# Two GpSimd instructions at other places, and the last returned rows taken in halves

## The reference

```
x = x + 0.5 * L0_ffn(layernorm(x))        # 8 experts, dense
x = x + L0_attn(layernorm(x))             # landmark attention
x = x + 0.5 * L0_ffn(layernorm(x))
x = x + 0.5 * L1_ffn(layernorm(x))        # 32 experts, top 4, plus a shared expert
x = x + L1_attn(layernorm(x), ...)        # windows of 128, half overlapping
x = x + 0.5 * L1_ffn(layernorm(x))
```

```
scores = softmax(flat @ router_w.T + router_bias)
topk_scores, topk_idx = top_k(scores, 4)                 # normalised over the 4
expert_out = (silu(gate_e x) * (up_e x)) @ down_e.T      # only the chosen 4 count
out = sum over the 4 of topk_score * expert_out
out = out + (silu(x @ sgate.T) * (x @ sup.T)) @ sdown.T  # the shared expert
```

## Time and profile before

| | us |
|---|---|
| median of 3 runs | 802.93 |
| lowest, highest | 802.22, 803.98 |
| the profiled execution | 803.43 |
| its span | 801.9 |

### The profile page before, as it was taken

How to read it: one execution, slowest core, us unless ns; L and a number is a source line. 1 busy time by engine, 2 the same in 40 slices (tenths; PEclk the granted TensorE clock), 3 DMA queues, 4 the chain that set the end, 5 groups by cost and what they waited for, 6 DMA issues and landing times.

```text
span 801.9 us, 19539 instructions
## 1 busy us (share of the span) xinstructions
PE 709.4 (88%) x6738; PEld 545.6 (68%) x6738; DVE 549.9 (69%) x1651; ACT 398.9 (50%) x967; POOL 442.8 (55%) x484
## 2 busy tenths in 40 slices
PE   7979998888999998898988889889968987988986
PEld 6868865556997756787777555557756775555655
DVE  6887477766886637987788745557588778555464
ACT  3656755565642553665652355562535423565531
POOL 4754560035650002655567677777237777777772
PEclk9998999999999999999999799999989898999999
DMA  8999999939003907300112454444301123444473
GB/s 226 206 204 202 203 200 207 214 84 205 6 4 67 165 2 268 126 1 33 40 46 66 117 130 113 113 119 145 119 12 48 45 67 99 108 112 112 110 230 112
DMA packets 121024, 93.99 MB, mean 117 GB/s; under 512 B 14176, under 2 KB 111840, under 8 KB 120544
## 3 DMA queue, kind: packets, MB, share of 16 engines
q1 hardware_dynamic: 104256, 70.00, 40.7%
q0 software_dynamic: 9216, 19.68, 7.1%
q10 hardware_dynamic: 7456, 3.07, 1.9%
HBM read 31.76 MB, written 57.41 MB: 111 GB/s over the span
## 4 chain that ended last, share of the span: by engine, by line
PE 37%; DVE 26%; issue 11%; POOL 11%; ACT 8%; ACTq 3%; DMA 3%; DVEq 0%; POOLq 0%; SPq 0%
PE banks L2046 6%; POOL sorted_rows L467 5%; POOL expert_rows L836 4%; PE banks L1424 3%; ACT routed_scratch L857 3%; DVE hT L1333 2%; PE banks L1027 2%; DVE rows_x L218 2%; DMA tile<-sorted_rows 2%; PE banks L414 2%; PE banks L416 2%; PE banks L415 2%; ACTq L894 2%; PE banks L1042 2%; POOL rstd L211 1%
## 5 line engine op out<-in xcount | busy, mean ns | idle before, releaser
L836 POOL DMA_INDIRECT expert_rows<-y,goal x160 | 154.5, 966 | 48.8 <-issue 46.2
L467 POOL DMA_INDIRECT sorted_rows<-rows_x,row_of x128 | 127.3, 995 | 66.1 <-issue 36.3
L1292 ACT ACTIVATE ys<-banks,wtab 128x128 f32<-128x128 f32 x256 | 73.3, 370 | 66.0 <-PE banks L1424 54.8
L1027 PE MATMUL banks<-routed_w,t 128*64 x320 | 82.2, 402 | 2.7 <-DVE t L921 1.8
L414 PE MATMUL banks<-x_high,w_high 128*128 128x512 f32 x192 | 83.9, 437 | 0.2 <-POOL w_low L1171 0.2
L1218 POOL TENSOR_TENSOR x<-ys,x 128x512 f32<-128x512 f32 x43 | 55.0, 1278 | 50.7 <-ACT ys L1292 50.4
L938 DVE TENSOR_TENSOR h<-sg,banks 128x512 f32<-128x512 f32 x40 | 27.5, 687 | 80.5 <-ACT sg L866 62.6
L1027 PE MATMUL banks<-routed_scratch,t 128*64 128x256 f32 x320 | 82.4, 403 | 0.0
L1424 PE MATMUL banks<-w,hT 128*128 128x128 f32 x512 | 71.7, 284 | 10.9 <-DVE hT L1333 10.7
L1424 PEld LDWEIGHTS banks<-w,hT 128*128 128x128 f32 x512 | 65.8, 195 | 19.8 <-issue 11.5
L211 POOL TENSOR_TENSOR rstd<-rstd,mhalf 128x4 f32<-128x4 f32 x24 | 26.7, 1114 | 91.9 <-DVE rstd L205 91.7
(11 more groups left out here) (361 smaller groups left out, 1717.2 us busy)
## 6 DMA issues: line engine op xcount, KB each, us to landing
sorted_rows<-zeros SPq DMA_DIRECT2D x32, 1120.0 KB, 17.9
tile<-sorted_rows SPq DMA_DIRECT2D x252, 35.0 KB
routed_w<-in_ffn_w SPq DMA_DIRECT2D x8, 768.0 KB, 11.9
w<-in_ffn_w SPq DMA_DIRECT2D x20, 192.0 KB, 5.2
routed_scratch<-expert_rows SPq DMA_DIRECT2D x3, 1024.0 KB, 5.7
expert_rows<-y,goal POOLq DMA_INDIRECT x160
tile<-sorted_rows ACTq DMA_DIRECT2D x68, 35.0 KB
qS<-x_high SPq DMA_DIRECT2D x8, 256.0 KB, 5.7
```

What stands on the lines that cost most here:

```text
L467: POOL.indirect_dma_start(sorted_rows, bass.IndirectOffsetOnAxis(self.row_of[:, g, i:i + 1], 0), rows_x[:, 4 * g + i // TOPK, :], None).th ...
L836: POOL.indirect_dma_start(expert_rows, bass.IndirectOffsetOnAxis(goal[:, 4 * q + i:4 * q + i + 1], 0), y[q % 6][:, i * P:(i + 1) * P], Non ...
L1027: last = PE.matmul(pairs(q)[ROWS * h:ROWS * h + ROWS, i, :], t[q % 2][:, rows], weights(q, i, h, slice(0, 2 * P)), start=True, stop=True)
L1292: last = SCL.mul(ys[s % 2][:, j * P:(j + 1) * P], bank[4 + s % 2][:, j * P:(j + 1) * P], wtab[:, t, e:e + 1])
```

## The change

Three things are changed, all of them in the stages after 567 us.

1. In `attn1`, POOL's `pool_pair(3)` stands ahead of `srt.norm.power(0)` and no longer behind it.
2. `pool_dispatch(1, 1)` becomes `pool_dispatch(1, 3)`: the power of group 2 stands behind three of group 1's indirect DMAs, not behind one.
3. In the second `Sorted`, the last group's returned rows are loaded in two DMAs of two tiles each, on two semaphores. DVE adds the shared expert's output first, and then sums each half when it is there; SP stores each half by itself.

```diff
@@ sync_engine of Sorted
                 SPLIT_AT = 12
+                LAST_HALVES = ((slice(0, 2), back_loaded[3]), (slice(2, 4), last_loaded))
...
                     if self.output is None:
                         load_back(2)
-                    load_back(3)
-                    if self.output is not None:
+                        load_back(3)
+                    else:
+                        rows = expert_rows[3 * TOPK * GW:4 * TOPK * GW, :].rearrange("(t p n) d -> p t (n d)", p=P, n=TOPK)
+                        for ts, half_loaded in LAST_HALVES:
+                            SP.dma_start(back[3][:, ts, :, :].rearrange("p t n d -> p t (n d)"), rows[:, ts, :]).then_inc(*half_loaded.inc)
                         self.store(2)
+                        for n, (ts, _) in enumerate(LAST_HALVES):
+                            SP.wait_ge(*combined(4 + n))
+                            SP.dma_start(self.output[:, 12 + ts.start:12 + ts.stop, :], x[:, 12 + ts.start:12 + ts.stop, :]).then_inc(*stored.inc)
...
@@ vector_engine of Sorted
-                        self.vector_sum(3, shared_next=True)
                         self.vector_shared_add(3)
+                        for ts, half_loaded in LAST_HALVES:
+                            self.vector_sum(3, ts, half_loaded(1))
...
-            def vector_sums(self, g, shared_next=False):
-                xg, b = x[:, 4 * g:4 * g + 4, :], self.back[g]
-                DVE.wait_ge(*self.back_here[g])
-                if not shared_next:
-                    DVE.wait_ge(*self.shared[g])
+            def vector_sums(self, g, ts=slice(0, 4), landed=None):
+                xg, b = x[:, 4 * g + ts.start:4 * g + ts.stop, :], self.back[g][:, ts, :, :]
+                DVE.wait_ge(*(landed or self.back_here[g]))
+                DVE.wait_ge(*self.shared[g])
...
                 DV(DVE.tensor_tensor(xg, half[:, :, 0, :], xg, ALU.add))
-                last = DVE.tensor_tensor(xg, half[:, :, 1, :], xg, ALU.add)
-                if shared_next:
-                    DV(last)
-                    self.combined[g] = self.shared[g]
-                else:
-                    last.then_inc(*combined.inc)
+                DVE.tensor_tensor(xg, half[:, :, 1, :], xg, ALU.add).then_inc(*combined.inc)
...
@@ pool_engine of attn1
                 norm.power(1)
                 earlier.pool_pair(2)
+                earlier.pool_pair(3)
                 srt.norm.power(0)
-                earlier.pool_pair(3)
                 srt.pool_dispatch(0, 8, (3, 9), norm)
-                srt.pool_dispatch(1, 1)
+                srt.pool_dispatch(1, 3)
                 srt.pool_dispatch(2, 1)
                 srt.pool_dispatch(3, 0)
...
@@ the end of the program
-        two.store(3)
-        SP.wait_ge(*stored(NG))
+        SP.wait_ge(*stored(NG + 1))
```

More of the change, by code:

```diff
@@ L403, in build @@
         dispatched_of = [dispatched] * (NG - 2) + [third_dispatched, last_dispatched]
+        last_loaded = signal("last_loaded", 16)
         pair_added, stored = signal("pair_added"), signal("stored", 16)
@@ L1111, in pool_pair, with vector_sum @@
                 POOL.tensor_tensor(self.pair[g], self.back[g][:, :, 2, :], self.back[g][:, :, 3, :], ALU.add).then_inc(*pair_added.inc)
-            def vector_sum(self, g, shared_next=False):
-                for _ in self.vector_sums(g, shared_next):
-                    pass
-            def vector_sums(self, g, shared_next=False):
-                xg, b = x[:, 4 * g:4 * g + 4, :], self.back[g]
-                DVE.wait_ge(*self.back_here[g])
-                if not shared_next:
-                    DVE.wait_ge(*self.shared[g])
-                half = routed.scratch[:, (36 + 8 * (g % 2)) * P:(44 + 8 * (g % 2)) * P].rearrange("p (t n d) -> p t n d", n=2, d=D)
+            def vector_sum(self, g, ts=slice(0, 4), landed=None):
+                for _ in self.vector_sums(g, ts, landed):
+                    pass
+            def vector_sums(self, g, ts=slice(0, 4), landed=None):
+                xg, b = x[:, 4 * g + ts.start:4 * g + ts.stop, :], self.back[g][:, ts, :, :]
+                DVE.wait_ge(*(landed or self.back_here[g]))
+                DVE.wait_ge(*self.shared[g])
+                half = routed.scratch[:, (36 + 8 * (g % 2)) * P:(44 + 8 * (g % 2)) * P].rearrange("p (t n d) -> p t n d", n=2, d=D)[:, ts, :, :]
                 DV(DVE.tensor_tensor(half, b[:, :, 0:2, :], b[:, :, 2:4, :], ALU.add))
```

## The result

The changed kernel's runs have a median of 800.13 us. Run beside them, the kernel before had a median of 808.55, and the ratio is 0.992 (95% interval 0.9893 to 0.9947, 20 runs each): 6.5 us less, between 4.3 and 8.7. The ratio is taken over the fast runs; the two medians are 8.4 us apart, inside the same interval. The forecast of 800.1 us meets the absolute time, and the direction is right, but that hides an error of size. I forecast a gain of 2.85 us from 802.93, and the three runs shown beforehand (802.22 to 803.98) lie low in what the kernel before does: over 20 runs, these three among them, it took 801.75 to 814.01.

The account below looks back on a forecast made before the run. POOL was taken as the bound from 624 us to the last scatter, beside a compute path ending 1.2 us before the loads. 0.72 + 1.4 + 0.73 = 2.85 us off 802.93 gave 800.1 us, range 798.8 to 801.6.

Parts of the forecast that it names:

- A: POOL's pair of group 3 ahead of group 0's power: DVE's normalisation of group 0 no longer slowed, gain 0.72 us.
- B: Power of group 2 behind three scatters of group 1: gain 2.0 us on POOL, 1.4 on PE.
- The delay p: Later end of group 2's power for the compute path: 0 to 0.4 us, taken as 0.1.
- DVE's L577 needs PE's L666, which ends at 646.56 + p: After group 3's normalisation, DVE's next instruction waits for a PE product, so the compute path gains 1.4 us, not 2.4.
- POOL's idle time ahead of group 3's scatters: Sign for B: POOL idle about 0.5 us before starting group 3's scatters.
- C: Last group's rows in two halves behind the shared add, at the program's end: 0.73 us beyond PE's gain.
- So the load no longer ends last; PE does.: At the end, PE finishes at 792.85 and the shared add at 793.6; the first half lands at 791.8.
- the rivals: Compute path keeps its place, 0.12; halves slow as whole loads, 0.08; PE's clock, 0.12; lower clock at the close, 0.05.
- that one goes away: Under the PE clock rival, the slow piece in 673 to 684 us vanishes: 798.4 us, chance 0.03.

Follow-up runs that it names:

- one whole load: The changed kernel with the last rows loaded, summed and stored as a whole behind the shared output; 802.69 us, ratio 0.996 to the kernel before.
- the whole again: The changed kernel with all three changes measured once more against the kernel before: 799.78 us, ratio 0.9901.
- C alone: The kernel before with only the last group in halves behind the shared output: 805.08 us, ratio 0.9947.
- PE kept busy: The kernel before with three unread products in PE's wait ahead of group 2's transposes: 807.51 us, ratio 1.0004.

## Why the size was wrong, step by step

**A, forecast 0.72.** The mechanism is as forecast: the pair fits into the hole and costs nothing there, though 1.6 us behind the other one. The size was too small, since I took 1.28 us for an undisturbed normalisation from group 3's row; this one took 1.11, and the gain is 0.88 (1.03 in the means, in which one execution of before with 13.46 stands).

**B, forecast 2.0 to 2.4 on POOL and 1.4 on PE.** POOL's part was nearly right: 2.37 between the two first traces up to the first quad (91.76 - 89.39), 2.77 in the means. Without the two traces in which POOL waited for the routing of group 3, the mean is 91.86, and B gives 2.52, two scatters at POOL's pitch. The delay p, taken as 0.1, was 0.03: behind group 0's power the power of group 2 ended at 42.84 before and 41.99 after, less A's 0.88; the power started at 624.85 and took 1.04, though DVE's x_low instruction ran until 624.96. The step that failed is the one for the compute path, "DVE's L577 needs PE's L666, which ends at 646.56 + p". It moved PE's row by p and took it as fixed otherwise. But that row was itself late by the piece at the lower clock in 628 to 636. With the piece, L666 ends 20.9 behind the power; without it 19.3, that is at 645.17 in the trace after, while DVE is at its normalisation until 645.9, where the copy starts, so it holds nothing back. By these rows, as an estimate: had the piece stayed, L666 would have ended 1.6 later, at 646.8, and DVE's copy would have come 0.9 later than it did, leaving the compute path 1.5 of B's 2.4: my 1.4. As it was, `row_of` of group 3 came 3.25 us earlier behind the power of group 0 (82.86 to 79.61), which is A's 0.88 and all of B's 2.37. My forecast for POOL's idle time ahead of group 3's scatters, 0.5 us, fails for the same reason: there is none but the issue gap. In all five traces with B the piece is gone or weak (0.79 in 624 to 632 with one whole load); why it goes with B, no run shows.

**C, forecast 0.73 beyond PE.** This is the term that was mis-sized most, and the sentence is "So the load no longer ends last; PE does." PE ended 4.13 us earlier behind the power of group 0 (212.08 to 207.95), not 2.1. Of this, 3.25 was won up to `row_of` of group 3; the other 0.88 lies behind it, in a distance that is 124.4 to 129.4 us in the traces without inserted work at the end, and no run places it. The load was issued only 2.1 earlier and not 2.7: of the 3.25 up to the first quad the 80 scatters took back 0.31 and the last one 0.84 (it took 1.79 us instead of 0.96). It was PE's gain that turned the answer: with the forecast 2.1 PE would have ended at 209.98 behind the power, later than the first half's 209.60. So the end stayed on the load's path, and there C gives its full price. My own numbers for that path were good: the first half there 4.1 us after its issue (measured 4.14), both half sums 3.15 (measured 3.12). Had I set the end by them, C was (5.74 - 4.1) + (3.40 - 3.15) = 1.9, and the measured 2.36 has the smaller store on top, 1.9 instead of 2.3 us behind DVE's last instruction. I had left this at zero.

By the Trainium skill (DMA: Bandwidth & Descriptors, "Anatomy of one DMA") the smaller store should save an estimated 0.3 us (2.6 for 256 KB, 2.3 for 128 KB). The page's fit is for transfers that GpSimd issues, and this one SP issues. From DVE's last instruction to the end of the span the traces show 2.3 to 2.4 us with the whole store and 1.8 to 1.9 with the half, so a saving of about 0.5, and both times lie below the page's.

**The sum.** Between the two first traces it is 0.88 + 2.37 - 0.31 - 0.84 + 2.33 = 4.43 us from the power of group 0 on; the two losses are the 80 scatters and the last one, which vary without the change too (100.7 to 103.6, and 2.3 to 3.1). By the means over the traces it is 1.03 + 2.77 + 2.36 = 6.2, and a further 0.8 in the 80 scatters (101.97 without B, 101.18 with it). Of this 0.8 a part is seen: in three of the five traces without B, POOL waits at the first quads for DVE's `goal`, up to 1.66 us at once, and in those with B the longest such wait is 0.59. The table's earlier `row_of` fits, but no run separates it from chance. 6.2 to 7.0 agrees with 6.5 and with the whole again (0.9901, 8.0 us, interval 5.5 to 10.4).

**The baseline.** The forecast subtracted from 802.93. Twenty runs of the same kernel have a median of 808.55. That the forecast time was met is the cancelling of two errors: a start 5.6 us too low, and a gain 5.6 us short of the 8.4 between the medians (3.6 short of the 6.5 by the ratio). That is luck. Of the rivals none occurred; the nearest is "that one goes away" of the third, but the piece that went was another one, and by the estimate above it counted by freeing DVE's copy, not by its own length.

**Still open.** The runs of the changed kernel had a mean granted clock of 0.972 and 0.974 (20 and 12 runs), those of before 0.968 (35 runs). Compared at equal clock (over these runs 0.01 goes with 5.5 us), the gain would be 4.4 us. That may take off too much, since whatever shortens a slow piece of PE raises this mean as well; the runs can't separate the two. 4.4 us is an estimate and no floor: it is above the forecast's 2.85 and agrees with the 4.43 between the two first traces, and the runs don't fix how much more the change is worth.

## What to carry to other kernels

Where two paths meet at the end, take the margin between them from several executions before choosing the one that sets the end; price the change on both, and say which error in the margin turns the answer. Take the time to subtract from as many runs as the kernel's spread asks for: here three runs lay 5.6 us under the median, twice the forecast gain. Where an experiment inserts work, read in its trace how long that work took: here it was nearly twice what was planned, and it moved what it should have left alone. Where the bound in a forecast is a row that lies behind a stretch at a lower granted clock, work it out a second time at the full clock, and put the difference into the range.

## What the runs showed of the hardware

- The same program took 801 to 816 us on two chips and 985 to 1005 on another, where the granted TensorE clock was 0.889 on average and POOL, the bound elsewhere, waited for DVE. What pays on one chip may pay less on the other; that the change does, no run shows.
- Runs of the kernel before beside the changed one spread over 12 us (801.75 to 814.01), and over all runs at this speed the time goes with the mean granted clock: 5.5 us for 0.01.
- A scatter's issue on POOL mostly took 0.96 us, and up to 1.8 where it started while a 128x1024 sum ran on DVE, as at 784.58 in the changed kernel's second trace:

```profile
784.33 1.22 DVE L1131 TENSOR_TENSOR routed_scratch<-rows_x 128x1024 f32<-128x1024 f32 x1
784.58 1.80 POOL L844 DMA_INDIRECT expert_rows<-y,goal  x1 [0.30 <-issue]
```

  Both sum inputs are in SBUF. In the last 110 us of the ten traces of the table 27 scatters started within such a sum, and every one ended 0.82 to 0.84 us behind the end of the sum: it took 1.76 to 1.80 us when it started 0.25 to 0.29 into the sum, 1.42 or 1.43 at 0.62, and 1.02 to 1.05 at 1.0. Which scatter is hit varies from execution to execution. In four of the ten it was the last one (after, C alone, PE kept busy, one whole load), and the load started 0.8 us later.
